# Fewer transfers for the stacks and the maxima, and another order of the steps without MLP, in four conditioned transformer blocks

## The reference, cut to what matters

```python
h = layernorm(x) * (1 + scale1) + shift1          # scale, shift, gate: from the condition, per sequence
q, k, v = heads(h @ Wq + bq), heads(h @ Wk + bk), heads(h @ Wv + bv)
attn = softmax(q @ k.T * s)                       # layer 1: causal; layer 2: s = 1, divided by 16 afterwards
x = x + gate1 * ((attn @ v) @ Wo + bo)
h = layernorm(x) * (1 + scale2) + shift2
x = x + gate2 * (gelu(h @ W1 + b1) @ W2 + b2)     # layers 0, 1 and 3
# layer 2 instead: h1 = attention(norm(x)) + x;  x = norm(h1) + h1
```

## Time and profile before

| | us |
|---|---|
| Median of 3 runs | 1169.81 |
| Lowest and highest run | 1166.87, 1176.10 |
| The profiled execution | 1167.0 |
| Its span, first to last instruction | 1165.2 |
| TensorE busy | 1066.8 (92%) |
| VectorE busy | 836.0 (72%) |
| ScalarE busy | 570.5 (49%) |
| POOL busy | 326.6 (28%) |
| Mean granted TensorE clock | 0.978 |

### The profile page before, as it was taken

One profiled execution on the slowest core, in us unless ns is written; L12 is line 12 of the kernel. 1 busy time (PEld: TensorE's weight loads), 2 busy tenths in 40 slices (PEclk: granted clock), 3 DMA queues, 4 the chain that ended last, 5 costly groups with the idle time before them and its releaser, 6 DMA issues.

```text
span 1165.2 us, 22743 instructions
## 1 busy us (share of the span) xinstructions
PE 1066.8 (92%) x8002; PEld 868.4 (75%) x8002; DVE 836.0 (72%) x2187; ACT 570.5 (49%) x1140; POOL 326.6 (28%) x408
## 2 busy tenths in 40 slices
PE   5789999999998999999999988888888999999987
PEld 4568888788886888888888755555656888788776
DVE  4477777777787877778787676666677777777743
ACT  4244565554553455545446444444445456555451
POOL 3033331233336333212333101111134333113332
PEclk9799999999999999999999998899889999999999
DMA  7732333222343235331233433333352133322300
GB/s 235 241 102 75 110 111 110 69 64 87 110 156 116 61 110 165 111 109 63 69 101 110 137 111 110 102 118 110 93 188 85 56 111 118 120 81 72 110 3 19
DMA packets 103279, 123.26 MB, mean 106 GB/s; under 512 B 9040, under 2 KB 96080, under 8 KB 102288
## 3 DMA queue, kind: packets, MB, share of 16 engines
q1 hardware_dynamic: 102608, 121.73, 33.2%
q10 hardware_dynamic: 576, 0.30, 0.1%
HBM read 85.16 MB, written 35.78 MB: 104 GB/s over the span
## 4 chain that ended last, share of the span: by engine, by line
PE 61%; DVE 13%; DMA 7%; issue 7%; ACT 5%; POOL 4%; SPq 1%; ACTq 0%; POOLq 0%; DVEq 0%
PE dense L1181 8%; PE o_banks L1331 8%; PE dense L1253 8%; PE s_bank L1278 7%; PE dense L1236 7%; DMA q_stack<-max_t 6%; PE st_bank L1315 5%; PE o_banks L1210 4%; DVE neg_max L865 3%; POOL hid_lo L522 3%; PE o_banks L1160 2%; PE o_banks L1339 2%; ACT probs L673 2%; PE o_banks L1196 2%; PE s_bank L1288 2%
## 5 line engine op out<-in xcount | busy, mean ns | idle before, releaser
L673 ACT ACTIVATE probs<-st_bank 128x512 f32<-128x512 f32 (+1 forms) x512 | 264.9, 571 | 167.8 <-PE st_bank L1315 116.6
L865 DVE TENSOR_REDUCE neg_max<-s_bank 128x2 f32<-128x512 f32 x384 | 255.3, 685 | 58.7 <-PE s_bank L1278 55.3
L1278 PE MATMUL s_bank<-k_stack,q_stack 96*128 96x256 f32 (+1 forms) x1024 | 228.7, 315 | 21.8 <-DMA k_stack<-qk_dram 10.3
L1278 PEld LDWEIGHTS s_bank<-k_stack,q_stack 96*128 96x128 f32 x1024 | 167.5, 195 | 63.9 <-DVE neg_max L865 21.6
L522 POOL TENSOR_TENSOR hid_lo<-hid,hid_hi 128x512 fp32r<-128x512 f32 x96 | 125.8, 1320 | 267.4 <-DVE hid_hi L977 267.4
L474 POOL TENSOR_TENSOR veps<-mv,eps_c 128x2 f32<-128x2 f32 x65 | 18.1, 278 | 511.0 <-DVE mv L831 511.0
L1315 PE MATMUL st_bank<-q_stack,k_stack 98*128 98x512 f32 x384 | 146.2, 452 | 14.9 <-DMA q_stack<-max_t 12.2
L661 ACT ACTIVATE hid<-dense,vec 128x256 f32<-128x256 f32 x192 | 80.6, 472 | 110.5 <-PE dense L1236 110.5
L1331 PE MATMUL o_banks<-probs,v_aug 128*32 128x256 f32 (+1 forms) x2048 | 123.8, 384 | 9.5 <-DVE xg L904 5.8
L1181 PE MATMUL dense<-ht,w_sb 128*128 128x256 f32 x512 | 127.7, 389 | 3.9 <-ACT ht L612 1.3
L1236 PE MATMUL dense<-ht,w_hi 128*128 128x256 f32 x384 | 116.4, 303 | 7.4 <-DVE ht_lo L970 6.2
(11 more groups left out here) (136 smaller groups left out, 1889.4 us busy)
## 6 DMA issues: line engine op xcount, KB each, us to landing
q_stack<-qk_dram SPq DMA_DIRECT2D x192, 128.0 KB, 2.9
k_stack<-qk_dram SPq DMA_DIRECT2D x96, 256.0 KB, 4.0
par_sb<-par_dram SPq DMA_DIRECT2D x32, 512.0 KB, 5.1
qk_dram<-q_hi SPq DMA_DIRECT2D x32, 256.0 KB, 2.1
qk_dram<-q_lo SPq DMA_DIRECT2D x32, 256.0 KB, 2.1
qk_dram<-k_hi SPq DMA_DIRECT2D x32, 256.0 KB, 2.2
qk_dram<-k_lo SPq DMA_DIRECT2D x32, 256.0 KB, 2.1
w_sb<-w SPq DMA_DIRECT2D x5, 1024.0 KB, 9.7
```

What stands on the lines that cost most here:

```text
L673: nc.scalar.activation(probs[p % 4][:, kt, :, q0:N], src, ACT.Exp, scale=SCORE_SCALE[l]).then_inc(p_sb, 1)
L865: nc.vector.tensor_reduce(neg_max[:, qt, 2 * p:2 * p + 2], split3(bank[:]), AX.X, ALU.max, negate=True).then_inc(s_max, 1)
L1278: ins = mm(bank[:, e * N:e * N + k1], q_stack[g.par][0:KB, 2 * p + e, qt * P:(qt + 1) * P].bitcast(F32R), k_stack[g.par][0:KB, p, 0:k1].bi ...
```

## The change

- `qk_dram` becomes (2, 2, 2, 128, 3, 256): for q and for k all three parts of a channel lie together. `spill` writes six times (each hi twice) and `stack` reads three times, 384 KB twice for q and 768 KB once for k.
- `max_rows` is one DMA for both parts, 16 KB from 16 partitions to 2. The counts of `max_ld`, `stack_ld`, `q_spill` and `k_spill` follow.
- The first eight tiles' `max_rows` go out on SyncE in all steps, at the end of the step before. The second eight's stay on ScalarE in steps without MLP.
- In steps without MLP, TensorE takes scores 10 to 15 between the products of the inputs, not behind them; the next inputs are turned (`ht1_early`, into `dense[1]`) before the first values and modulated then; ln1 moves before and around the first residual on VectorE; the split of the first eight maxima comes before `out_norm` and the modulation; `max_turn(a, 0)` comes before `ao_turn`.
- POOL has `power` and `pick` of n first in such steps (behind `split_w1`).

```diff
-    qk_dram = nc.dram_tensor("qk_dram", (2, 4, KT, P, N), F32).ap()
+    qk_dram = nc.dram_tensor("qk_dram", (2, 2, KT, P, 3, N), F32).ap()
...
+        def inputs_ready(g):
+            return g.off > 0 and not has_mlp(g.back(1))
...
-            for part in range(2):
-                dst = q_stack[g.par][KB + part:KB + part + 1, h0:h0 + H // 2, :]
-                src = max_t[half][part * H // 2:(part + 1) * H // 2, :]
-                eng.dma_start(dst, src).then_inc(max_ld, 16)
+            dst = q_stack[g.par][KB:KM, h0:h0 + H // 2, :]
+            eng.dma_start(dst, max_t[half][:]).then_inc(max_ld, 16)
...
+                for which, hi, hi_sb, lo, lo_sb, spilled in ((0, q_hi, q_hi_sb, q_lo, q_lo_sb, q_spill),
+                                                             (1, k_hi, k_hi_sb, k_lo, k_lo_sb, k_spill)):
+                    dst = qk_dram[a.par, which].rearrange("t p c n -> p t c n")
+                    wait(sp, hi_sb, a.count(1, 1))
+                    for c in (0, 1 + which):
+                        sp.dma_start(dst[:, :, c], hi[:]).then_inc(spilled, 16)
+                    wait(sp, lo_sb, a.count(1, 1))
+                    sp.dma_start(dst[:, :, 2 - which], lo[:]).then_inc(spilled, 16)
...
+                rows = [qk_dram[a.par, which].rearrange("t (j r) c n -> (r c) (t j) n", j=4) for which in range(2)]
+                wait(sp, q_spill, a.count(48, 48))
+                for e in range(2):
+                    half = slice(e * 3 * HD, (e + 1) * 3 * HD)
+                    dst = q_stack[a.par][half].rearrange("r (p e) n -> r p e n", e=2)[:, :, e, :]
+                    sp.dma_start(dst, rows[0][half]).then_inc(stack_ld, 16)
+                wait(sp, k_spill, a.count(48, 48))
+                sp.dma_start(k_stack[a.par][0:KB], rows[1]).then_inc(stack_ld, 16)
...
-                if a.exists and HAS_MLP[g.layer]:
+                if a.exists:
                     max_rows(sp, a, 0)
...
+                if not mlp and n.exists:
+                    power(n, 0, ln1_mv, ln1_veps, ln1_rstd)
+                    wait(pool, ht1_sb, n.count(1, 0))
+                    pool.wait_ge(mod_cols, 2 * (n.layer + 1))
+                    pick(n, 0, mod1_now)
...
@@ ScalarE, step without MLP @@
+                    query_hi(a)
+                    exps(g, 0)
+                    key_hi(a)
+                    exps(g, 1)
+                    value_copy(a)
+                    exps(g, 2, 3)
                     max_rows(act, g, 1)
+                    modulate1(n, dense[1])
                     out_copy(g, 0)
+                    exps(g, 4, 5, 6, 7)
                     out_copy(g, 1)
...
@@ VectorE, step without MLP @@
-                    if inputs:
-                        query_lo(a)
-                        key_lo(a)
-                    maxima(g, 10, 11, 12, 13, 14, 15)
+                    maxima(g, 10, 11)
+                    query_lo(a)
+                    maxima(g, 12, 13)
+                    key_lo(a)
+                    maxima(g, 14, 15)
                     max_split(g, 1)
+                    ln1_a(n)
                     max_copy(g, 1)
+                    wait(dve, ln1_stats, n.count(1, 1))
+                    norm_mv(0, ln1_mv)
                     if c.exists:
                         first_residual(c)
+                    ln1_c(n)
...
+                    maxima(a, 0, 1, 2, 3, 4, 5, 6, 7)
+                    max_split(a, 0)
                     out_norm(g, 1)
                     if modulated:
                         modulation_cols(modulated)
-                    maxima(a, 7)
-                    max_split(a, 0)
                     max_copy(a, 0)
...
@@ TensorE @@
+            def ht1_early(n):
+                wait(pe, xn1_done, n.count(1, 1))
+                wait(pe, k_lo_sb, n.count(1, 0))
+                transposed(dense[1], xn1, ht1_ps)
...
@@ TensorE, step without MLP, after score(g, 8, 9) @@
+                    q_product(a, 0)
+                    score(g, 10)
+                    q_product(a, 1)
+                    score(g, 11)
                     score_t(g, 0)
+                    k_product(a)
+                    score(g, 12)
                     score_t(g, 1)
+                    v_product(a, 0)
+                    score(g, 13)
+                    v_product(a, 1)
+                    score(g, 14)
                     score_t(g, 2)
+                    score(g, 15)
+                    score_t(g, 3)
                     if c.exists:
                         projection(c, 0)
                     max_turn(g, 1)
-                    score_t(g, 3)
                     if c.exists:
                         projection(c, 1)
...
+                    ht1_early(n)
                     values(g, 0)
...
-                    score(a, 4)
+                    score(a, 4, 5)
                     score_t(g, 7)
-                    score(a, 5)
+                    score(a, 6)
...
                     values(g, 1)
-                    score(a, 6)
+                    score(a, 7)
                     out_turn(g, 1)
-                    score(a, 7)
+                    max_turn(a, 0)
                     ao_turn(g)
-                    if n.exists:
-                        ht1_t(n)
-                    max_turn(a, 0)
```

More of the change, by code:

```diff
@@ L260, in inputs_of, with has_mlp @@
             return a.exists and (a.reg is not None or a.off > 0)
+        def has_mlp(g):
+            c = g.back(1)
+            return c.exists and HAS_MLP[c.layer]
+        def inputs_ready(g):
+            return g.off > 0 and not has_mlp(g.back(1))
         def modulation_of(g):
@@ L348, in spill @@
             def spill(a):
[L349 to L356, removed]
-            def stack(a):
[L359 to L369, removed]
@@ L380, in step @@
                 if not mlp:
-                    wait(sp, max_ld, g.count(64, 64))
+                    wait(sp, max_ld, g.count(32, 32))
                 if g.reg is None:
@@ L443, in _ @@
             load_weights(0, O_2, WCOLS, w2_ld)
+            max_rows(sp, Step(0), 0)
             run_steps(sp, step, after)
@@ L526, in step @@
                 c, a, n = g.back(1), g.ahead(1), g.ahead(2)
-                if inputs_of(a):
+                mlp = has_mlp(g)
+                if inputs_of(a) and not inputs_ready(g):
                     pool.wait_ge(mod_cols, 2 * (a.layer + 1))
@@ L531, in step @@
                     pick(a, 0, mod1_now)
-                mlp = c.exists and HAS_MLP[c.layer]
                 if g.reg is None and g.off == 0:
@@ L580, in hi_part @@
             def hi_part(a, which, ps, bank, dst, done, spilled):
-                wait(act, spilled, a.count(32, 0))
+                wait(act, spilled, a.count(48, 0))
                 wait(act, ps, a.count(1, 1))
@@ L676, in step @@
             def step(g):
-                c, a = g.back(1), g.ahead(1)
-                inputs, mlp = inputs_of(a), c.exists and HAS_MLP[c.layer]
-                if inputs:
-                    modulate1(a)
+                c, a, n = g.back(1), g.ahead(1), g.ahead(2)
+                inputs, mlp = inputs_of(a), has_mlp(g)
+                if inputs and not inputs_ready(g):
+                    modulate1(a, o_bank[1])
                 if mlp:
@@ L723, in _ @@
             first = Step(0)
-            modulate1(first)
+            modulate1(first, o_bank[1])
             query_hi(first)
@@ L880, in max_copy @@
                 wait(dve, max_ps, g.count(2, half + 1))
-                wait(dve, max_ld, g.count(64, 32 * half + 32 - 64))
+                wait(dve, max_ld, g.count(32, 16 * half + 16 - 32))
                 nc.vector.tensor_copy(max_t[half][:], s_bank[half % 2][0:H, 0:N]).then_inc(max_sb, 1)
@@ L885, in lo_part @@
                 l = a.layer
-                wait(dve, spilled, a.count(32, 0))
+                wait(dve, spilled, a.count(48, 0))
                 wait(dve, ready, a.count(1, 1))
@@ L1264, in score @@
                     if j == 0:
-                        wait(pe, stack_ld, g.count(144, 144))
+                        wait(pe, stack_ld, g.count(48, 48))
                         wait(pe, s_max, g.count(16, 0))
```

59 lines of the change are left out of this document (13 added, 46 removed).

## The result

| | before | after |
|---|---|---|
| Median, us | 1172.55 (4 runs) | 1196.26 (4 runs; 1190.7 to 1205.3) |
| Ratio, 95% interval | | 1.022 [1.017, 1.027] |
| Profiled execution and its span | 1167.0, 1165.2 | 1190.9, 1189.1 |
| Mean granted clock | 0.978 | 0.964 |

What follows compares the result with a forecast made beforehand. MLP steps were taken as TensorE-bound, steps without MLP as bound by engine-to-engine waits. Gains 11.7 + 3 + 4 + 1.5 less 2 made 18.2 us, from a median of 1169.8 to 1151.6, stated as 1150; range 1131 to 1170.

Steps and rivals of the forecast that it cites:

- The order, nine steps at 1.3 us: Steps without MLP (0, 17 to 24): earlier score_t(4) and shorter step end gain 1.3 us each, 11.7 over nine.
- rival (c): Layer 2: the clock stays up, four falls of 2.61 us go, 10.4 us more gain, 1139 us; chance 0.13.
- The failed step: Steps without MLP: the 768 KB k_stack load takes 5.5 us, landing just before score(a,0); the row's 0.66 us gain is cancelled.
- six issues fewer: SyncE's queue: three stack issues, about 1.9 us, replace nine; rows and par_sb land earlier in MLP steps.
- MLP steps, 4 us gained: Steps with MLP: a shorter SyncE queue takes 4 of TensorE's 7.2 us of row waits; bounds 0 and 7.2.
- Steps 0 and 17, 3 us: Steps with a modulation behind the last maxima: earlier split and modulation columns gain 3 of 4.03 us of TensorE waits.
- The start, 1.5 us: First scores, waiting 7.99 us for k_stack: fewer issues on SyncE's queue gain 1.5 us; bounds 0 and 3.8.
- Layer 3's weights, 2 us: Steps 23 and 24: weight loads go out some 13 us later behind max_rows(a,0), costing 2 us; bounds 0 and 5.
- Clock, zero: Layer 2's steps without MLP: four clock falls before and four after, so 0 us.
- Rival (d): Steps without MLP: a second thin stretch brings 18 clock falls instead of four, +18 us, 1185; chance 0.12.
- the signs of a wrong prediction: Steps without MLP: ht1_early waits over 1.5 us, values not before +14.2, stack wait at score(a,0), PEclk at most 0.89 in over five.
- The signs for the order: Layer 2: steps near 27.3 us, sum near 231, no q_lo wait, max_t copied near +11.0, ao turn last.

Runs made afterwards that it cites:

- Run 9: Kernel before with the new order, old stack transfers, k_lo moved ahead of maximum 13 and the row as one DMA: 1155.13 us, ratio 0.985 to before.
- run 1: Changed kernel with its transfers as before (four spills, nine loads, two row DMAs), so only the order is new: 1184.25 us, ratio 1.016 to before.
- Run 4: Changed kernel with stacks loaded in nine DMAs, each to every third partition, from the new DRAM layout, six spills kept: 1186.68 us, ratio 1.014 to before.
- run 10: Changed kernel, new order and new transfers, with only k_lo moved ahead of maximum 13: 1184.63 us, ratio 1.013 to before.
- Run 7: Changed kernel with stacks loaded in nine DMAs, each to neighbouring partitions, from the new DRAM layout: 1271.44 us, ratio 1.083 to before.

## Why the prediction was wrong

I said 1150 with a range to 1170 and 0.11 for slower. The range was also narrower than my own terms allow: with the lower bound of each, the sum is a loss of 7 us, 1177. Point by point:

- **The order, nine steps at 1.3 us.** Right as a mechanism, on one condition that I passed over, and in size for five steps of the nine. Run 9 does each of steps 19 to 23 in 27.6 us where I had 27.3; values at +14.19 (I had +13.95), score_t(4) at +16.05 (+15.8). The condition is that row and stack are there. A full-clock step was 28.6 before, so the order gives 1.0 us there; the rest of what run 9 gains in these five steps, 138.11 against 150.99 us, is clock falls that did not come, my rival (c). Steps 17 and 18 gained next to nothing (32.19 and 32.26 us, first score to first score), and step 24 lost 3.5.
- **The failed step** is the one of the stacks: "Issued at about +11, it lands at +16.5, just when score(a,0) wants it at +16.9. So I give the 0.66 us back to this traffic, and keep nothing of it here. Bounds: 0.66 gained, 1.9 lost in a step." Three things in it were wrong. The load took 7.9 us, not 5.5 as my interpolation between 4.0 and 8.4 had it; its upper end was nearly right, and nothing was saved by parts that overlap. I set its landing against score(a,0) and allowed the row of score_t(4), which shares the DMA engines, only the 0.66 us: that DMA took 7.32 us instead of 3.46, and score_t(4) starts at +18.90 instead of +15.8. Even my 1.9 us for a lost step was too little. And my slack of 0.4 us was not there, since without the new loads k_lo's later place alone breaks it (run 1).
- **What I took for a saving, six issues fewer, is no saving.** The nine issues of 0.63 us were spacing. The loads landed beside the issues that followed, so much of their bytes was through when the row came. Run 4 shows it with the new layout: nine spaced loads, and a row wait of 0.4 us in place of 17.0.
- **MLP steps, 4 us gained.** The row waits went from 4.2 (the 2.4 of the earlier trace rows and 1.8 at L1315, in layer 0, which I had left out) to 1.6 us in 76 to 640, and the stack waits rose from 1.8 to 11.0. So the first score of step 17 is 3.9 us late where I had a gain. From 890 us on the row waits fell from 4.8 to 2.0, and the stack waits rose from 0.5 to 3.7. I had looked at the queue of issues and not at score(a,0) in these steps.
- **Steps 0 and 17, 3 us.** The wait of the earlier trace rows fell from 3.10 to 1.0 us in step 0 and from 0.93 to 0.3 in step 17, as I had it, but the steps are no shorter. Step 0 takes 44.51 us against 44.45 (42.29 in run 9). In step 17 the row took it back, 1.4 us at score_t(4), and the clock fell with it: this one step is 7.8 us longer, more than steps 19 to 23 together.
- **The start, 1.5 us.** Nothing: first score at 31.87 against 31.67, with k_stack issued at 24.07 and 7.8 us of landing. My upper bound of 3.8 counted issues that the landing hides.
- **Layer 3's weights, 2 us.** There, and larger: POOL waits 11.9 us once for w_sb, the rstd of step 24 comes behind it, and TensorE waits 3.7 us for xn. In run 9, where the stacks cost least, step 24 is 3.5 us longer than before; in after it is 6.4, with 2.0 us more for the stack.
- **Clock, zero.** Wrong. Layer 2's busy time is 6.3 us more than before, and all of that and more is in steps 17 and 24. Rival (d) named 1185 and a second thin stretch in the order. It came close in time and is not the cause: run 9 has the same order and the same thin stretch, and steps 19 to 23 at full clock. The clock fell in steps where a wait for a DMA came on top of it, but not by its length: 1.21 us of wait came with 2.77 us of busy time in run 1, 2.77 with 1.2 in step 19 of after, and 1.87 with none in run 10. In sum over steps 19 to 23, after against run 9, such waits were paid twice, 9.8 us as waits and 9.5 as clock.

Of the signs of a wrong prediction, ht1_early's wait (1.69 us) and values not before +14.2 came; the wait at score(a,0) came in run 1, while in after the row's, which I had not named, stands ahead of it. PEclk was at or below 0.89 in three steps (0.82, 0.80, 0.85), not in more than five. The signs for the order came: no wait for q_lo, the copy ended at +11.5, the ao turn is last. The row waits in MLP steps, to be under 3 us, are 3.6.

What remains open: why neighbouring partitions are slow. The Trainium skill, page "DMA: Bandwidth & Descriptors", section "The descriptor swizzle", maps four neighbouring partitions (and the four that lie 32 higher) to one SBUF port. By an estimate from that, 16 neighbouring partitions are written through 4 ports, and 16 partitions three apart through eight or more. Run 7 against run 4 agrees in direction (4.9 against 3.1 us, 7.6 against 4.2); that the ports are the cause is an inference, and no run here separates it from other causes. In after, with 48 and 96 rows in one DMA, this effect and the closer issue act together, and their shares were not separated. Open too is how the row is held (the last section), and why a wait takes the clock down in one step and not in another.

## What to carry to other kernels

Before merging DMAs, ask who else is waiting for the DMA engines in that interval: here 1.5 MB of loads issued within 2 us held back a small urgent transfer on another queue until they were all but in, and nine issues with every third partition as destination left it gaps. Nine to neighbouring partitions did not (run 7), so look at the destination as well as at the size. Merge the small urgent one first (here worth 1%), and keep the large ones spaced. When an order is rewritten, follow each producer of a late transfer, not only the engines' own chains: one vector operation 1.4 us earlier was worth 2.0%, since a wait of TensorE can also take the clock down, and that can cost more than the wait itself. And sum the steps of a profile one by one before explaining a typical one: two thirds of the 21.0 us stood in steps 17 and 24.

## What the hardware showed that I had not expected

- A 16 KB DMA on ScalarE's queue took 7.32 us behind 1.5 MB of loads on SyncE's, and none of its packets ran in the first 5 us. The Trainium skill, page "DMA: Bandwidth & Descriptors", section "Queues, rings and completion order", has each DMA engine alternate between the queues for which it has work, packet by packet; by an estimate from that rule the row would have been in after a few packets of each engine. This trace shows no such alternation for 5 us. It doesn't tell whether the row's packets stood ready meanwhile or were only made later, so it isn't shown which part held them. In run 4, with the engines' share at 63 to 79% in place of 112%, the row's packets ran among q1's, some 2 us after its issue.
- The same 119534 packets and 138.66 MB took 30% more of the DMA engines' time when the destination partitions of each load, and its source rows, were neighbours (47.1% of 1271.6 us against 38.5% of 1195.0: 0.080 and 0.062 us a packet), and the kernel took 6.8% more by the ratios.
- 27 unread matmuls in each of the seven steps without MLP and modulation made the kernel 0.6% faster.
